# One tile's value product moved from the fourth block to the third, whole, with sums of its own, in an attention and expert-layer kernel

## The reference

```
h = layernorm(x)                                  # per token
for each sequence and each of 16 heads (D = 16):  # 64 heads in all
    self  = softmax(causal(q k^T / 4)) v          # 512 x 512, keys = own tokens
    cross = softmax(qc kc^T / 4) vc               # 512 x 1601, keys = context rows
x = x + tanh(g_xattn) * ((self + cross) Wp + bp)
h = layernorm(x)
x = x + tanh(g_ffn) * (shared_expert(h) + top-2 of 7 routed experts(h), weighted)
```

## Time and profile before

| | us |
|---|---|
| median of three timed runs | 1357.56 (1357.21 to 1358.14) |
| the profiled execution | 1360.2 |
| its span, first to last instruction | 1358.4 |
| TensorE busy | 1318.3 (97%) |
| VectorE busy | 870.6 (64%) |
| ScalarE busy | 731.4 (54%) |
| Pool busy | 374.2 (28%) |
| share of the 16 DMA engines, SyncE's queue | 25.9% |
| mean granted TensorE clock | 0.987 of 2.4 GHz |

### The profile page before, as it was taken

How to read it: one execution, slowest core, us unless ns; L and a number is a source line. 1 busy time by engine, 2 the same in 40 slices (tenths; PEclk the granted TensorE clock), 3 DMA queues, 4 the chain that set the end, 5 groups by cost and what they waited for, 6 DMA issues and landing times.

```text
span 1358.4 us, 22060 instructions
## 1 busy us (share of the span) xinstructions
PE 1318.3 (97%) x7336; PEld 651.1 (48%) x7337; DVE 870.6 (64%) x1749; ACT 731.4 (54%) x1101; POOL 374.2 (28%) x609
## 2 busy tenths in 40 slices
PE   7989999999999999999999999899999999999996
PEld 4645333333333333333333333355556777777775
DVE  6778888888888889888888888446321222222221
ACT  4644777777777777777777777531111222222221
POOL 5555211231232232312322223110001333333331
PEclk9999899999999999999999999999998999999998
DMA  7764222322322323323223224156031221111121
GB/s 238 227 205 163 83 77 77 107 97 72 124 86 88 115 78 97 108 71 112 90 88 116 78 95 153 59 215 261 1 104 40 34 35 31 31 31 31 31 32 22
DMA packets 80265, 129.10 MB, mean 95 GB/s; under 512 B 15728, under 2 KB 50288, under 8 KB 79152
## 3 DMA queue, kind: packets, MB, share of 16 engines
q1 hardware_dynamic: 71600, 117.72, 25.9%
q0 software_dynamic: 7296, 9.97, 4.5%
q10 hardware_dynamic: 1280, 0.27, 0.1%
HBM read 82.17 MB, written 45.36 MB: 94 GB/s over the span
## 4 chain that ended last, share of the span: by engine, by line
PE 88%; DMA 2%; DVE 1%; ACT 1%; SPq 1%; issue 1%; POOL 0%; POOLq 0%; ACTq 0%; DVEq 0%
PE ps L746 20%; PE ps L629 14%; PE ps L896 13%; PE ps L728 13%; PE ps L909 7%; PE ps L848 6%; PE ps L859 4%; PE ps L731 3%; PE ps L920 2%; PE ps L641 2%; DMA k_parts<-work 1%; PE ps L637 1%; PE ps L702 1%; PE ps L824 1%; PE ps L886 1%; DMA arena<-rowst 1%
## 5 line engine op out<-in xcount | busy, mean ns | idle before, releaser
L1358 DVE TENSOR_REDUCE mx<-ps 128x1 f32<-128x512 f32 (+3 forms) x960 | 576.6, 648 | 79.3 <-PE ps L629 79.3
L1065 ACT ACTIVATE arena<-ps 128x1024 f32<-128x1024 f32 (+1 forms) x512 | 485.8, 989 | 124.0 <-PE ps L728 116.2
L746 PE MATMUL ps<-arena 128*32 128x512 f32 (+5 forms) x2432 | 291.0, 525 | 0.6 <-ACT arena L1065 0.6
L1255 POOL TENSOR_SCALAR_AFFINE_SELECT arena<-arena 128x128 f32<-128x128 f32 x256 | 74.8, 292 | 510.8 <-ACT arena L1065 501.8
L629 PE MATMUL ps<-arena 96*128 96x512 bf16 x576 | 203.9, 384 | 5.3 <-DMA arena<-k_parts 2.9
L728 PE MATMUL ps<-arena 98*128 98x512 bf16 x624 | 198.5, 381 | 1.4 <-ACT arena L1065 1.0
L896 PE MATMUL ps<-arena,work 128*128 x608 | 186.4, 460 | 0.5 <-issue 0.5
L1665 DVE TENSOR_TENSOR work<-work,ps 128x352 f32<-128x352 f32 x76 | 39.6, 521 | 179.1 <-ACT work L1142 179.1
L896 PEld LDWEIGHTS ps<-arena,work 128*128 128x128 f32 x608 | 112.5, 190 | 57.4 <-issue 1.1
L629 PEld LDWEIGHTS ps<-arena 96*128 96x128 bf16 x576 | 55.5, 96 | 171.8 <-DVE mx L1358 115.0
L1142 ACT ACTIVATE work<-ps 128x352 f32<-128x352 f32 x76 | 35.2, 463 | 167.8 <-PE ps L896 167.8
(11 more groups left out here) (172 smaller groups left out, 1428.7 us busy)
## 6 DMA issues: line engine op xcount, KB each, us to landing
arena<-in_experts SPq DMA_DIRECT2D x8, 2176.0 KB, 16.8
o_parts<-work SPq DMA_DIRECT2D x63, 256.0 KB, 7.7
arena<-k_parts SPq DMA_DIRECT2D x48, 198.1 KB
arena<-k_parts SPq DMA_DIRECT2D x48, 132.1 KB
k_parts<-work SPq DMA_DIRECT2D x16, 300.0 KB, 4.4
q_parts<-work SPq DMA_DIRECT2D x12, 384.0 KB, 4.4
arena<-q_parts SPq DMA_DIRECT2D x48, 96.0 KB
work<-recip_rows SPq DMA_DIRECT2D x16, 256.0 KB
```

The source lines that it names most:

```text
L746: mm = pe.matmul(ps[32 * q:32 * q + VW, 6, b0:b1], vst[0:kn, r % VR, TT + kt if cross else kt, :], pr[0:kn, c0:c0 + b1 - b0], start=(phase ...
L1065: act.activation(pr[:, c0:c0 + n], ps[:, 2 * (g % 2):2 * (g % 2) + 2, :].rearrange("p b n -> p (b n)")[:, 0:n], ACT.Exp, scale=SCALE).then ...
L1255: pool.affine_select(out=exps, in_=exps, pattern=[[1, P]], compare_op=ALU.is_ge, fill=0.0, base=0, channel_multiplier=-1).then_inc(S["mask ...
L1358: return dve.tensor_reduce(m, out, AX_X, ALU.max)
```

## The change

The last context tile, X12, is no longer cut. Its exponentials move from group 7 to group 5, where they take the place of Y2 and Y3, which go to group 7. Its value product runs whole in the third block, in the fourth strip, into a bank of the ring (in place of one of the two spare entries). ScalarE copies these sums (`rest_out`) at the end of the head's step, SyncE stores them as a fifth group of rows, and they are loaded and added as a fifth denominator and numerator. The products of Y2 and Y3 stand last in the fourth block. Pool's masks 2 and 3 wait for group 7 and stand last in Pool's step. The copy of the main sums has two buffers. Two waits on the loads are moved or added behind the heads (ScalarE before its second shared-expert tile, VectorE before the third sequence's norm).

The diff, cut:

```diff
-          [(X, 6, 0), (X, 7, 512)], [(X, 8, 0), (Y, 2, 512), (Y, 3, 768)], [(X, 9, 0), (X, 10, 512)],
-          [(X, 11, 0), (X, 12, 512)]]
+          [(X, 6, 0), (X, 7, 512)], [(X, 8, 0), (X, 12, 512)], [(X, 9, 0), (X, 10, 512)],
+          [(X, 11, 0), (Y, 2, 512), (Y, 3, 768)]]
...
-          [(X, 6), (X, 7), (X, 8), (Y, 2)], [(X, 9), (X, 10), (X, 11), (Y, 3), (X, 12)]]
+          [(X, 6), (X, 7), (X, 8), (X, 12)], [(X, 9), (X, 10), (X, 11), (Y, 2), (Y, 3)]]
...
-MASKS_BY = [1, 2, 3, TT]
-REST_CUTS = [(0, 172), (172, 342), (342, T)]
+MASKS_BY = [1, 2, 2, TT]
...
-MASKED = [(0, 1), (1, 3), (2, 5), (3, 5)]
+MASKED = [(0, 1), (1, 3), (2, 7), (3, 7)]
...
+NQ = 5
+CROSS, SELF, REST_SUMS = (0, 1, 2), 3, 4
...
         if g == 3:
-            out += [("spare", 0), ("values", 0)]
+            out += [("spare",), ("values", 0)]
         if g == 5:
-            out += [("spare", 1), ("values", 1)]
+            out.append(("values", 1))
         if g == 7:
-            out.append(("values", 2))
+            out += [("rest",), ("values", 2)]
...
-ENTRIES = [item for item in PE_ORDER if item[0] in ("max", "spare")]
+ENTRIES = [item for item in PE_ORDER if item[0] in ("max", "spare", "rest")]
...
-        osb = work[:, 2 * T:3 * T]
+        osb = [work[:, (2 - i) * T:(3 - i) * T] for i in range(2)]
+        restsb = [shared[:, (4 + i) * T:(5 + i) * T] for i in range(2)]
...
+            def rest_store(v):
+
+                sp.wait_ge(S["rest_evac"], v + 1)
+                sp.dma_start(o_parts[v, P:P + D + 1, :], restsb[v % 2][P - VW:P - VW + D + 1, :]).then_inc(rest_written[v % 2], 16)
...
                 heads = o_parts[bass.ds(j * GH + h0, h1 - h0)]
-                for q in range(4):
+                for q in range(NQ):
...
                 if h == 3:
                     num_load(j, 1)
+                    num_load(j, 2)
                 if h == 4:
-                    num_load(j, 2)
-                    num_load(j, 3)
+                    num_load(j, SELF)
+                    num_load(j, REST_SUMS)
                 if h == 5:
                     recip_load(j)
+                rest_store(u)
                 sums_store(u)
...
+                if before[0] == "rest" and step >= 0:
+                    pe.wait_ge(S["rest_evac"], step + 1)
...
+                for cross, kt in PHASES[phase]:
+                    c0 = WHERE[cross, kt]
+                    if cross and kt == CT - 1:
+                        mm = pe.matmul(bank_of("rest")[P - VW:P, :], vst[0:CTAIL, r % VR, TT + kt, :], pr[0:CTAIL, c0:c0 + T],
+                                       start=True, stop=True, skip_group_check=True)
...
+                        if item[1] == 2:
+                            bank_free(u, "rest")
...
+            def rest_out(u):
+
+                act.wait_ge(S["pv_done"], u * NPH + 3)
+                if u >= 2:
+                    act.wait_ge(rest_written[u % 2], 16 * (u // 2))
+                act.activation(restsb[u % 2][P - VW:P, :], bank_of("rest")[P - VW:P, :], ACT.Copy).then_inc(S["rest_evac"], 1)
...
             def sums_out(u):
 
+                v = u - 1
                 act.wait_ge(S["pv_done"], u * NPH)
-                if u > 1:
-                    act.wait_ge(S["o_written"], u * 16 - 16)
-                act.activation(osb[:, :], ps[:, 6, :], ACT.Copy).then_inc(S["o_evac"], 1)
+                if v >= 2:
+                    act.wait_ge(o_written[v % 2], 16 * (v // 2))
+                act.activation(osb[v % 2], ps[:, 6, :], ACT.Copy).then_inc(S["o_evac"], 1)
...
                     if g == 2 and nxt2:
                         diag_out(u)
+                rest_out(u)
...
                 pool.tensor_tensor(den[:, 0, :], den[:, 0, :], den[:, 1, :], ALU.add).then_inc(S["den_half"], 1)
+                pool.tensor_tensor(den[:, 2, :], den[:, 2, :], den[:, REST_SUMS, :], ALU.add).then_inc(S["den_third"], 1)
...
                 pool.tensor_tensor(y, y, cross_num[0], ALU.add).then_inc(S["num_half"], 1)
+                pool.tensor_tensor(cross_num[1], cross_num[1], cross_num[2], ALU.add).then_inc(S["num_third"], 1)
...
                 mask(u, 1, 2)
-                mask(u, 2, TT)
                 if nxt2:
                     diag_mask(u + 2)
...
                 if h == OUT_IN:
                     outputs(group)
+                mask(u, 2, TT)
```

More of the change, by code:

```diff
@@ L251, in program @@
         rowst = sb("rowst", [MROWS * 2 * TT, P], BF16)
[L252 removed]
+        osb = [work[:, (2 - i) * T:(3 - i) * T] for i in range(2)]
         DW = T // D
[L254 to L255 removed]
+        restsb = [shared[:, (4 + i) * T:(5 + i) * T] for i in range(2)]
+        den = work[:, 0:NQ * DW].rearrange("p (q t) -> p q t", q=NQ)
+        recip = work[:, NQ * DW:(NQ + 2) * DW].rearrange("p (s t) -> p s t", s=2)
         cross_recip, self_recip, self_num = [work[:, i * T:(i + 1) * T] for i in (3, 4, 5)]
[L257 removed]
+        cross_num = [shared[:, 6 * T:7 * T], shared[:, 7 * T:8 * T], region("wq")[:, 0:T]]
         wr_cols = sb("wr_cols", [P, 2, VW])
@@ L344, in program @@
         gathered = [S["gathered0"], S["gathered1"]]
+        o_written = [S["o_even"], S["o_odd"]]
+        rest_written = [S["rest_even"], S["rest_odd"]]
         block = ctx.enter_context(nc.Block())
@@ L525, in sums_store @@
                 sp.wait_ge(S["o_evac"], v + 1)
-                sp.dma_start(o_parts[bass.ds(v, 1)].rearrange("a p t -> (a p) t"), osb).then_inc(S["o_written"], 16)
+                sp.dma_start(o_parts[v, 0:P, :], osb[v % 2]).then_inc(o_written[v % 2], 16)
+            def rest_store(v):
+                sp.wait_ge(S["rest_evac"], v + 1)
+                sp.dma_start(o_parts[v, P:P + D + 1, :], restsb[v % 2][P - VW:P - VW + D + 1, :]).then_inc(rest_written[v % 2], 16)
             def den_load(j, h0=0, h1=GH):
                 sp.wait_ge(S["parts_free"], j + 1)
-                sp.wait_ge(S["o_written"], j * (16 * GH) + 16 * h1)
+                for i in range(2):
+                    sp.wait_ge(o_written[i], 16 * ((j * GH + h1 + 1 - i) // 2))
+                    sp.wait_ge(rest_written[i], 16 * ((j * GH + h1 + 1 - i) // 2))
                 heads = o_parts[bass.ds(j * GH + h0, h1 - h0)]
-                for q in range(4):
+                for q in range(NQ):
                     src = heads[:, VW * q + D:VW * q + D + 1, :].rearrange("u a (d t) -> (u a) d t", t=DW)
@@ L580, in _ @@
             den_load(NGRP - 1, 0, GH - 2)
-            for q in range(4):
+            for q in range(NQ):
                 num_load(NGRP - 1, q, 0, GH - 2)
+            rest_store(NU - 2)
             sums_store(NU - 2)
             den_load(NGRP - 1, GH - 2, GH - 1)
-            for q in range(4):
+            for q in range(NQ):
                 num_load(NGRP - 1, q, GH - 2, GH - 1)
+            sp.wait_ge(S["rest_evac"], NU)
+            sp.dma_start(cross_num[2][P - D:P, :], restsb[(NU - 1) % 2][P - VW:P - VW + D, :]).then_inc(S["num_in"], 16)
             sp.wait_ge(S["o_evac"], NU)
-            for q, dst in enumerate([yT[:, NGRP - 1, :], *cross_num, self_num]):
-                sp.dma_start(dst[P - D:P, :], osb[VW * q:VW * q + D, :]).then_inc(S["num_in"], 16)
+            for q, dst in enumerate([yT[:, NGRP - 1, :], *cross_num[0:2], self_num]):
+                sp.dma_start(dst[P - D:P, :], osb[(NU - 1) % 2][VW * q:VW * q + D, :]).then_inc(S["num_in"], 16)
             recip_store(NGRP - 1)
@@ L739, in values @@
                 pe.wait_ge(S["masked"], u * TT + MASKS_BY[phase])
[L740 to L747, removed]
+                for cross, kt in PHASES[phase]:
[3 more added lines that the diff above has]
+                                       start=True, stop=True, skip_group_check=True)
+                    else:
+                        first = 0 if cross else kt * P
+                        q = kt % 3 if cross else SELF
+                        mm = pe.matmul(ps[32 * q:32 * q + VW, 6, first:T], vst[:, r % VR, TT + kt if cross else kt, :],
+                                       pr[:, c0:c0 + T - first], start=(phase == 0),
                                        stop=(phase == NPH - 1), skip_group_check=True)
@@ L1084, in _ @@
             act.wait_ge(S["o_evac"], NU)
-            for q in range(4):
-                src = osb[VW * q + D:VW * q + D + 1, :].rearrange("a (d t) -> a d t", t=DW)
-                act.dma_start(den[P - D:P, q, :], src).then_inc(S["den_in"], 16)
+            for q in range(NQ):
+                src, row = (restsb[(NU - 1) % 2], P - VW + D) if q == REST_SUMS else (osb[(NU - 1) % 2], VW * q + D)
+                act.dma_start(den[P - D:P, q, :], src[row:row + 1, :].rearrange("a (d t) -> a d t", t=DW)
+                              ).then_inc(S["den_in"], 16)
             def xn_out(b):
@@ L1532, in _ @@
             shared_hidden(0, 0, 1)
+            dve.wait_ge(S["num_in"], 16 * NQ * (NGRP + 2))
+            dve.wait_ge(S["den_in"], 16 * NQ * (NGRP + 2))
             second_norm(2 * TT, 3 * TT)
```

20 lines of the change are left out of this document (11 added, 9 removed).

## The result

The changed kernel takes 1380.8 us (median of four runs, 1378.16 to 1383.37), the kernel before 1357.38 on the same chip: ratio 1.0179, 95% interval 1.0162 to 1.0196. It is 24 us slower. The direction was forecast, the size was not: 1363.6 was said, with a range to 1372. The profiled execution took 1378.16 us, its span is 1376.1; that is 17.7 us more than the span of before.

A forecast was written before the change was run, and what follows sets the result against it. The loop from the third block through VectorE's or ScalarE's and Pool's chain to the transpose L669, then TensorE, was taken to bound the kernel. Terms 2.4 - 0.5 + 3.5 + 0.6 = +6.0 us gave 1363.6 us, range 1355.5 to 1372.

The forecast's parts named there:

- The fourth block: TensorE's fourth value block shrinks by 0.30 us to 0.99; off the loop, so 0 gained (bounds 0 and -18.3 us).
- The bank's wait: Third block waits for VectorE to empty its ring bank; with the longer product 0.04 us a step, 2.4 us in all.
- second queue slot: Third block's bank wait: a further wait might take a second queue slot, giving the upper bound of 0.12 us a step.
- ScalarE's copy: Copy of the new sums fits ScalarE's idle time before the Exp, over at about 504.10: cost 0, at most 0.1 a step.
- rival D: ScalarE's copy ends later than 504.20 and delays the Exps on the loop: 6 us more, 1369.7 us; chance 0.10.
- The masks: Pool's masks of the last two own tiles come late but in time: cost 0; steps of 11.59 us vanish, -0.5 us.
- rival E: Pool's diagonal mask doesn't move earlier, so outputs and sums hold the masks: 19 us, 1382 us; chance 0.06.
- The denominators: In one step of eight, Pool's masks wait behind the fifth load and additions: 0.5 us times 7, 3.5 us.
- Two buffers, the extra stores and loads: Second buffer for the main sums gains nothing; extra DMA of 34 KB a head, 256 KB a group costs 0.
- The end: Last value block also waits for two masks, and ScalarE has 0.3 us more copies: +0.6 us.
- B: Same loop, but neither new wait bites (bank free in time, fifth load lands with the others): 1357.7 us; chance 0.22.

The follow-up runs named there:

- experiment 4: Kernel before without the value products of the last context tile's three pieces (its 65 rows left out of the sums): 1356.52 us, ratio 1.0006.
- experiment 5: Changed kernel with the small store at 32 rows, and only the last context tile's product waiting for its bank: 1356.51 us, ratio 1.0001 to the kernel before.
- a_rows32: Changed kernel with the fifth group of sums stored as 32 rows instead of 17: 1360.95 us, ratio 1.0036 to the kernel before.
- a_late: The kernel of experiment 5: changed kernel, 32-row store, bank wait only before the last context tile's product: 1356.51 us, ratio 1.0001 to the kernel before.
- experiment 3: Kernel before with one more store a head from a constant tile, of 24 rows (1356.54 us, ratio 1.0000) or 34 rows (1382.88 us, ratio 1.0200).
- b_store24: Kernel before with one more store of 24 rows (48 KB) a head from a constant tile: 1356.54 us, ratio 1.0000.
- b_store17: Kernel before with one more store of 17 rows (34 KB) a head from a constant tile: 1384.71 us, ratio 1.0213.

## Why the prediction was wrong

By its own steps:

1. The fourth block: right. 0.99 instead of 1.29 us, worth nothing on the loop (experiment 4), and the transpose waits for VectorE as said.
2. The bank's wait: right. The step is 11.48 (11.47 said), 61 x 0.045 = 2.7 us (2.4 said), and PEld has the wait 61 times, longest 0.3. The wait's place makes 0.02 of the 0.045 (experiment 5). No row shows the second queue slot that the upper bound of 0.12 assumed.
3. ScalarE's copy: right. It runs at 273.06, is over at 273.65 and the Exp behind it starts at 273.78; rival D didn't come.
4. The masks: right. No step is lengthened by a late VectorE instruction beside Pool's copy, and rival E didn't come: the diagonal's mask ran 0.15 us behind the second mask's end.
5. The denominators: right in kind, too large. Said 3.5 us for seven groups. The steps concerned have 1.2 us too much in `a_rows32`, 0.4 in `a_late`. The term that was mis-sized is the landing: Pool's first addition waits for all five loads, so its start shows when the fifth is there. Counted from the transpose before it, that is a mean of 7.82 us before and 8.14 in `a_rows32`, 0.3 later where I had put 0.8.
6. **Two buffers, the extra stores and loads: this is the step that failed.** "34 KB a head, ... DMA is a quarter busy. 0." It cost 18.8 us of steps in the profiled execution, and 20 us between the medians of the two kernels with 17 and 32 rows. I priced bytes against a mean over 16 engines. The store has 17 rows, goes to one of them, and puts 34 KB a head there, while the 256 KB of the main sums put 256 / 16 = 16 KB on each. And that one already had, by the estimate of experiment 3, 202 KB a head of queries and keys. Everything that is cut over all 16 lands with its slowest share, so the main store went from 7.7 to 11.0 us and some of SyncE's issues grew to 2 us.
7. The end: not as said. From the last transpose to the end of the span it is 1358.4 - 850.72 = 507.7 us before, 1376.1 - 869.46 = 506.6 after, and 1359.7 - 853.01 = 506.7 in `a_rows32`: 1 us less, where I said 0.6 more. That can't be told from nothing: in kernels whose end no edit touches it goes from 504.6 us (`b_store24`) to 507.7 (before). In `a_rows32` the wait for the masks is there (1.42 us before the last block) and is made up behind it; I didn't follow where.

So the sum of the other six parts holds: 1363.6 was said, 1360.95 measured with a store that spreads. In part that is luck: part 5 was 2.3 us too large, part 7 can't be read, and the measured 4.9 us may be 3.1 to 6.8 by its interval. None of my rivals had a DMA that slows others; B has only the landing of the fifth load. I had looked at the new wait and the new copy in tenths of a microsecond and given the new transfer one sentence; its bound from above was never worked out. The number of rows stood in the diff, and the page of the Trainium skill named under experiment 3 gives the rule that would have made it a rival.

What stays open: why only the steps h = 6, 7 and 0 of a group are long, when the small store comes in every head. They follow the group's loads (sums and reciprocals): of the loads of queries and keys, those issued from h = 3 on take longer, up to 16.7 us for those issued in h = 6, and three steps later they are back at 11. So it seems that the overloaded engine falls behind there and catches up later; but no run separates the group's loads from the store.

## What to carry to other kernels

Price a DMA by its longest share, not by its bytes: the rows of the slowest dimension, divided by the largest number up to 16 that divides them. Then add up what the other transfers' shares put on the same engine: here the small store came behind a share of every load of queries and keys. 17 rows cost 29 us where 24 or 32 cost 0 to 1.5; rounding up to padding that nobody reads is the cheap way out. A mean DMA share of 26% says nothing of this; the landing time of a neighbour's transfer (from 7.7 to 11.0 us, but only to 9.2 in `b_store17`) and the length of the queue's issues do.

Before shortening a block, look at what the first instruction behind it waits for. If an engine that doesn't depend on the block is late there by as little as 0.05 us, shortening is worth nothing (18 us of work removed, 0 gained), and moving one ready product in front of the wait is worth 4 (ratio 0.9971, 0.9955 to 0.9986).

## What was not expected of the hardware

A transfer of 34 KB in one share slows transfers that have nothing to do with it: loads of keys reach TensorE up to 1.9 us late, and SyncE's issue of one store goes from 0.28 to 2.11 us. Two shares of 17 rows (+27 us) stand beside one (+29 us; intervals 1.0183 to 1.0217 and 1.0189 to 1.0238): no difference can be told. The semaphores' records fit that: in both kernels the small store lands 0.9 to 1.3 us behind the keys, and by the estimate there two engines carry the same 202 KB of queries and keys. So it seems that only how far behind the slowest engine is matters, not how many are.
